# Gelu twice on ScalarE, rounded and in full, in place of a rounding pass on GpSimd, in a chain of three conditioned transformer layers

## What is computed

```python
xn2 = _ln(x) * (1 + sc_mlp[:, None, :]) + sh_mlp[:, None, :]
h = jax.nn.gelu(xn2 @ w1 + b1, approximate=True)     # approximate=False in the third layer
x = x + g_mlp[:, None, :] * (h @ w2 + b2)
```

## Time and profile before

| what | value |
|---|---|
| median of three runs | 4482.74 us |
| profiled execution, its own time | 4479.91 us |
| its span | 4478.2 us |
| TensorE busy, matmuls | 4131.2 us (92%) |
| VectorE busy | 3626.3 us (81%) |
| ScalarE busy | 2290.5 us (51%) |
| GpSimd busy | 1113.3 us (25%) |
| `M_gelu` L707 on ScalarE | 480 passes, 266.6 us |
| `M_hh` L621 on GpSimd | 480 passes, 280.7 us |

### The profile page before, as it was taken

The page is one execution under the profiler, slowest core; times in us unless marked ns, Lnnn a source line. Parts: engine busy times, 40 slices in busy tenths (PEclk is TensorE's granted clock), DMA queues, the critical chain, the costliest instruction groups (busy, mean ns, idle before and its releaser), DMA issues. The chain is left out here.

```text
span 4478.2 us, 124730 instructions
## 1 busy us (share of the span) xinstructions
PE 4131.2 (92%) x46329; PEld 3534.8 (79%) x46329; DVE 3626.3 (81%) x7651; ACT 2290.5 (51%) x3893; POOL 1113.3 (25%) x2051
## 2 busy tenths in 40 slices
PE   6764899999999999999999999999999999999998
PEld 4653788888888887888888888877888888888886
DVE  5775888988889897777777777789888888888885
ACT  1212555555555555555555555555555555555553
POOL 1002222222222232322222222223222222222222
PEclk7576999999999999999999999999999999999999
DMA  3101111011110111111111110111110111010110
GB/s 81 23 1 56 31 28 32 25 32 29 30 32 25 32 42 51 38 28 32 27 30 32 28 32 25 32 44 54 27 28 26 28 26 30 24 33 22 33 26 22
DMA packets 124773, 142.33 MB, mean 32 GB/s; under 512 B 16974, under 2 KB 120308, under 8 KB 124640
## 3 DMA queue, kind: packets, MB, share of 16 engines
q1 hardware_dynamic: 124496, 140.27, 12.0%
q10 hardware_dynamic: 144, 0.22, 0.0%
HBM read 111.40 MB, written 29.06 MB: 31 GB/s over the span
## 5 line engine op out<-in xcount | busy, mean ns | idle before, releaser
L1024 DVE TENSOR_REDUCE mx<-S 128x4 f32<-128x1024 f32 x768 | 903.1, 1217 | 167.5 <-PE S L1266 160.1
L759 ACT ACTIVATE pT<-S 128x1024 f32<-128x1024 f32 x768 | 745.5, 1023 | 368.6 <-PE S L1294 368.6
L707 ACT ACTIVATE hf<-M 128x512 f32<-128x512 f32 (+1 forms) x480 | 266.6, 556 | 738.3 <-DVE hl L1015 387.4
L621 POOL TENSOR_SCALAR hh<-hf 128x512 fp32r<-128x512 f32 (+1 forms) x480 | 280.7, 585 | 833.2 <-ACT hf L707 785.4
L1294 PE MATMUL S<-qT,kT 32*128 32x256 f32 x9216 | 424.1, 295 | 17.7 <-ACT pT L759 14.7
L1307 PE MATMUL A<-pT,V 128*32 128x256 f32 x6144 | 412.0, 386 | 25.3 <-ACT pT L759 25.3
L1294 PEld LDWEIGHTS S<-qT,kT 32*128 32x128 f32 x9216 | 327.6, 184 | 88.7 <-issue 46.9
L1201 PE MATMUL A<-wqkv_hi,xh 128*128 128x288 f32 x1152 | 282.6, 327 | 108.2 <-DVE x L1071 90.3
L1346 PE MATMUL M<-xh,w_hi 128*128 128x256 f32 x1728 | 364.6, 292 | 1.2 <-POOL xh L595 1.2
L1385 PE MATMUL M<-w_lo,hh 128*128 128x288 f32 x1728 | 352.6, 303 | 0.0
L1346 PE MATMUL M<-xh,w_lo 128*128 128x256 f32 x1728 | 344.5, 280 | 0.0
(11 more groups left out here) (246 smaller groups left out, 9786.3 us busy)
## 6 DMA issues: line engine op xcount, KB each, us to landing
mid<-xbo SPq DMA_DIRECT2D x64, 288.0 KB, 4.0
xld<-mid SPq DMA_DIRECT2D x64, 288.0 KB, 3.8
xa<-mid SPq DMA_DIRECT2D x64, 288.0 KB, 3.6
gA<-gates SPq DMA_DIRECT2D x96, 144.0 KB, 3.4
gM<-gates SPq DMA_DIRECT2D x96, 144.0 KB, 3.7
xld<-in_x_dram SPq DMA_DIRECT2D x32, 288.0 KB, 3.9
xa<-in_x_dram SPq DMA_DIRECT2D x32, 288.0 KB, 3.5
out_dram<-xbo SPq DMA_DIRECT2D x32, 288.0 KB, 2.2
```

Source lines behind the costliest of these rows:

```text
L621: pool.tensor_scalar(hh[:, 2 * f:2 * f + m, :].rearrange("p m c -> p (m c)"), hf[:, f % 3, 0:m * T], 1.0, 0.0, ALU.mult, ALU.add).then_inc ...
L707: act.activation(hf[:, f % 3, 0:c], MBANK[f % 2][:, 0:c], gelu(n)).then_inc(s["m_hf"], 1)
L759: act.activation(pT[:, g % 2, 2 * h:2 * h + 2, :], S[:, 2 * h:2 * h + 2, :], ACT.Exp, scale=float(HD) ** -0.5).then_inc(s["a_ex"], 1)
L1024: dve.tensor_reduce(mx[:, p, :, :], S[:, r:r + 2, :].rearrange("p a (t k) -> p a t k", t=NT), AX.X, ALU.max).then_inc(s["a_mx"], 1)
```

## The change

ScalarE applies gelu twice to each chunk: first into `hh`, whose type fp32r rounds it as it is written, then in full into the ring `hf`. GpSimd's `M_hh` goes. The wait for `m_y` (the old `hh` has been used) moves to ScalarE's first gelu, and `M_hl` waits for the second gelu (`m_hf`).

```diff
-            def M_hh(n, f):
-
-                wait(pool, "m_y", n, 0)
-                wait(pool, "m_hf", n, f + 1)
-                m = min(2, FM - 2 * f)
-                constant_wait(pool)
-                pool.tensor_scalar(hh[:, 2 * f:2 * f + m, :].rearrange("p m c -> p (m c)"), hf[:, f % 3, 0:m * T],
-                                   1.0, 0.0, ALU.mult, ALU.add).then_inc(s["m_hh"], 1)
-
...
                 if m is not None:
-                    M_hh(m, 0)
-                    M_hh(m, 1)
                     swap(nxt, 3, (8,))
                     M_residual(m)
-                    M_hh(m, 2)
                     swap(nxt, 3, (9, 10))
-                    M_hh(m, 3)
-                    M_hh(m, 4)
                 swap(nxt, 1, (3,))
...
                 if f == 0:
                     wait(act, "m_xl", n, 1)
+                    wait(act, "m_y", n, 0)
                 if f >= 3:
                     wait(act, "m_hl", n, f - 2)
-                c = T * min(2, FM - 2 * f)
+                m = min(2, FM - 2 * f)
+                c = T * m
+                act.activation(hh[:, 2 * f:2 * f + m, :].rearrange("p m c -> p (m c)"), MBANK[f % 2][:, 0:c], gelu(n)).then_inc(s["m_hh"], 1)
                 act.activation(hf[:, f % 3, 0:c], MBANK[f % 2][:, 0:c], gelu(n)).then_inc(s["m_hf"], 1)
...
             def M_hl(n, f):
-                wait(dve, "m_hh", n, f + 1)
+                wait(dve, "m_hf", n, f + 1)
```

## The result

The changed kernel takes 4540.97 us (median of four runs, 4537.33 to 4544.06); the kernel before, run beside it, 4482.84 us. The ratio is 1.013, with a 95% interval of 1.0115 to 1.0146. It is slower, as I had forecast, but by 58 us and not by 168; the time lies inside the range, near its lower end. The profiled execution took 4540.36 us with a span of 4538.3 us.

A forecast was written before the change was run, and what follows sets the result against it. A loop of VectorE's chain and TensorE bounds the slot. Profiled 4479.9 us, plus 171 (94 slots of 1.82), less 3, gives 4648, or 4651 us on the median; range 4505 to 4690 us.

The forecast's parts named there:

- What bounds the kernel, and what moves: VectorE's chain and TensorE bound the slot; M_residual starts right behind A_v's copies and delays M_xl: 171 us in all.
- I take 1.82 us: Loss per slot if GpSimd's L611 and L613 go ahead of VectorE's L946 and L947; 94 slots give 171 us.
- the seam: Profiled place where two L603 copies, then at once L422, kept L946 waiting until 0.54 us after L422; GpSimd went first.
- 171 - 3: Forecast change in us: 171 lost as M_residual meets M_xl, 3 gained from fewer GpSimd passes.
- The first rival: VectorE's L946 goes before L611, only L947 waits: 0.42 us a slot, 39 us, 4516 us; chance 0.27.
- The room: Slack of VectorE's chain before TensorE's first scores, A_scores(0): between 0 and 0.15 us, taken as 0.1.
- the forecast's 1.92 us: Delay of L947's end in a slot, from 2040.26 to 2042.18, before 0.1 us of room is taken off.
- Rows 10 and the seams: VectorE's subtractions waited 5.9 us for GpSimd's roundings, mostly in the last items; gain 0 to 5.9 us, taken as 3.
- ScalarE at nothing: 480 more ScalarE passes, 267 us on an engine 51% busy, cost nothing; upper bound 10 us.
- the second rival: Not slower: gM lands late, M_residual starts after L947, slots unchanged, 4477 us; 0.13 with all else leaving slots alone.

The follow-up runs named there:

- The experiment that did the move alone: Kernel before, GpSimd's rounding kept and ScalarE untouched, with only M_residual moved ahead of M_hh(0) and M_hh(1): 4539.7 us, ratio 1.013.
- the one that undid it: Changed kernel with M_residual again held back until the second chunk's second gelu, both gelu passes kept: 4485.53 us, ratio to before 1.0005.
- the last two kernels: Changed kernel with loops cut to one pass, 4666.43 us; the same with M_residual's three waits put ahead of A_v's copies, 4544.73 us.

## Why the prediction was right and wrong

- **What bounds the kernel, and what moves.** Right. L611 starts as the second copy ends (in the first layer's loop behind L935), it and M_xl exclude each other, and the delay goes by the scores to the slot, in the written-out slots by the low products as well. The experiment that did the move alone and the one that undid it have the whole loss between them.
- **The step that failed**: "I take 1.82 us, since the seam has the same two copies and the same L946 followed by a GpSimd operation with waits already met". I put a written-out slot's order into every slot. In the loops VectorE goes ahead of L611: there L936 waits (second and third layer, 0.34 us a slot) or, later on, the copies of L1041 do (first layer, 0.39 us), and of 95 distances 75 are of these two kinds. The price was close where it applied: 1.72 us more in a written-out slot between the seams, and 166 us between the two kernels that are written out throughout, where I had 171 - 3.
- **The first rival** had the slots right in two loops of three (0.42 us forecast, 0.34 measured in the second and third layer), and its 4516 us lacks what the written-out slots lose more. (It stands on the profiled execution's time; on the median, as the forecast's 4651, it would be 4519 us.) I gave it 0.27; the answer was a mixture, which neither case allowed for. What would have told me: the two kinds of code were in the trace of before, from a loop and the earlier trace rows from a seam, and no row showed a loop's slot with a third GpSimd instruction behind the copies. I should have priced the two kinds apart, or held the order open for the loops.
- **The room.** I took 0.1 us at the scores. It is 0.18 us at the reciprocals, and next to nothing at the scores: L1255 starts 0.15 us after the last L998 has ended, as before, though it is released late. With 0.18 the forecast's 1.92 us give 1.74 a slot, and 1.72 were measured.
- **Rows 10 and the seams.** The 3 us that I took off were not to be seen: VectorE's subtractions wait 6.4 us for gelu now where they waited 5.9 for GpSimd.
- **ScalarE at nothing.** Right in the loops. At the seams the profiled execution of the run that undid the move keeps some 7 us, of which the last section follows 3.3 to GpSimd's queue and the clock; the rest stays open.
- **What I had not seen**: the copies in SBUF (L1041). With M_residual a little later they, and not the subtractions, would have made the loss, and a larger one. "It meets only operations that read PSUM" in the second rival was wrong: had `gM` landed late, the time would have been about that of the run that holds M_residual for M_xl, 4574 us, and not 4477.

## What to carry to other kernels

An instruction that waits also keeps everything behind it in its queue away from other engines: before one is taken out of GpSimd's list, look at what it held back and which of VectorE's operations between SBUF tiles, copies among them, that will meet. Where two engines exclude each other, price both orders, and separately for looped and written-out code. Time won on an engine off the path is worth something only when work from the path is put there.

## What was not expected of the hardware

**Who goes first is mostly steady, but not by start times.** In the changed kernel the slots of one loop go alike (but for the first layer's first), and the written-out ones the other way; three waits in another place turned the written-out ones round (4666 and 4545 us). The Trainium skill (SBUF — State Buffer, "Who interferes with whom") has the order of issue decide; the two slots above from the run with six more written out, alike in their starts and opposite in their order, do not show that. Nor do the last two kernels: the subtraction starts 0.15 to 0.16 us behind the first copy in nearly every slot of the one with GpSimd ahead, and in most slots of the one with VectorE ahead as well. What does decide stays open.

**A clock that falls at the seams.** In the run that undid the move, the last two slots ahead of the second layer are 1.5 and 1.8 us longer than before. Its timelines of VectorE, GpSimd and TensorE in the second of them:

```profile
1722.63 2.49 DVE L1005 TENSOR_TENSOR hl<-hf,hh 128x512 fp32r<-128x512 f32 x2
```
```profile
1723.02 1.55 POOL L422 TENSOR_TENSOR wo_lo<-wst,wo_hi 128x576 fp32r<-128x576 f32 x1 [4.55 <-ACT wo_hi L415]
```
```profile
1725.63 0.50 PE L1191 MATMUL A<-wqkv_hi,xh 128*128 128x288 f32 x2 [2.21 <-DVE x L1061]
...
1728.37 0.68 PE L1191 MATMUL A<-wqkv_hi,xh 128*128 128x288 f32 x2
```

Without the roundings ahead of it GpSimd's splitting of weights, too, comes earlier and meets two subtractions (2.49 us; 1.28 in the same slot before). TensorE then waits 2.21 us, where it waited 0.99, and soon after runs pairs of products in 0.68 us in place of 0.43, at a granted clock of 0.50 (1727 to 1730 us). In the other of the two slots TensorE's longest wait is 1.15 us in both kernels, and here the clock falls all the same; the windows of that run just before and in that stretch (span, busy time of PE, PEld, DVE, ACT, POOL, granted clock):

```profile
1680.00:1682.40 2.40, 0.51 (x8) 0.30 (x8) 2.37 (x5) 0.95 (x3) 0.00 (x0) 1.00 0.00 0
1682.40:1684.00 1.60, 1.55 (x6) 1.58 (x7) 1.46 (x4) 1.19 (x2) 0.00 (x0) 0.53 0.00 0
```

TensorE had been busy 0.51 of 2.40 us, and the granted clock behind it was 0.53, about the lower level (1.2 of 2.4 GHz). Over this whole slot it was 1.00 in the kernel before and is 0.96 here. At the same place of the kernel before (1680.00 to 1682.30 us) TensorE was busy 0.51 of 2.30 us, and the clock stayed at 1.00. Why it fell in this kernel and not in that one was not tried.
